# Reordering the lists of three engines in the first dispatch block of a layer-norm, linear-attention and soft-mixture kernel

## The reference

```
o   = (q k^T / sqrt(C)) v          # no softmax; q, k, v from a layer-normed x
x   = x + ln(ln(x) + o proj + b)   # first sublayer
x3  = ln(x)                        # second sublayer
logits   = einsum('bmd,dnp->bmnp', x3, phi)           # 64 experts x 32 slots
dispatch = softmax(logits, axis=0)                    # over the batch of 2
combine  = softmax(logits over n*p)
slots = einsum('bmd,bmnp->bnpd', x3, dispatch)
y     = einsum('bnpd,nde->bnpe', slots, W) + b
out   = einsum('bnpd,bmnp->bmd', y, combine)
x     = x + ln(out)
```

## Time and profile before

| | us |
|---|---|
| median of 3 runs | 640.99 |
| lowest and highest run | 640.54, 641.14 |
| the profiled execution | 641.88 |
| its span, from the first to the last instruction | 640.1 |
| PE busy | 628.2 |
| DVE busy | 447.9 |
| ACT busy | 359.0 |
| POOL busy | 230.2 |

### The profile page before, as it was taken

One profiled execution on the slowest core, in us unless ns is written; L12 is line 12 of the kernel. 1 busy time (PEld: TensorE's weight loads), 2 busy tenths in 40 slices (PEclk: granted clock), 3 DMA queues, 4 the chain that ended last, 5 costly groups with the idle time before them and its releaser, 6 DMA issues.

```text
span 640.1 us, 15341 instructions
## 1 busy us (share of the span) xinstructions
PE 628.2 (98%) x5351; PEld 395.4 (62%) x5351; DVE 447.9 (70%) x857; ACT 359.0 (56%) x694; POOL 230.2 (36%) x410
## 2 busy tenths in 40 slices
PE   8999999999999999999999999999999999999996
PEld 8898644545444444444444457777777777777776
DVE  5978888835244453446344399999888888888886
ACT  5666776843233232224444356777777777777764
POOL 5375896820000000000000001555555555555554
PEclk9999999999999999999999999999999999999999
DMA  8920032325766666666555531222222222222201
GB/s 266 402 77 1 1 67 50 67 60 156 201 176 176 177 193 185 173 178 203 135 136 186 159 104 67 91 90 90 90 90 90 90 90 90 90 90 90 90 16 34
DMA packets 78485, 77.07 MB, mean 120 GB/s; under 512 B 6386, under 2 KB 74995, under 8 KB 76147
## 3 DMA queue, kind: packets, MB, share of 16 engines
q1 hardware_dynamic: 76112, 74.48, 38.4%
q10 hardware_dynamic: 2338, 2.16, 1.0%
HBM read 51.71 MB, written 23.07 MB: 117 GB/s over the span
## 4 chain that ended last, share of the span: by engine, by line
PE 79%; DVE 8%; POOL 5%; issue 3%; DMA 2%; ACT 2%; SPq 1%; DVEq 0%; POOLq 0%; ACTq 0%
PE psL L1568 24%; PE psM L1555 11%; PE psL L1687 11%; PE psM L1705 7%; PE psM L1709 7%; PE psM L1706 7%; PE psM L1585 3%; POOL small L492 2%; DMA r_xn<-in_proj_wT 2%; PE psL L1773 1%; PE psL L1453 1%; PE psM L1511 1%; DVE phs L1091 1%; DVE small L1286 1%; DVE r_xn L1305 1%
## 5 line engine op out<-in xcount | busy, mean ns | idle before, releaser
L1568 PE MATMUL psL<-r,r_xn 128*128 128x512 f16 x768 | 176.3, 379 | 0.8 <-DVE r L1112 0.8
L1568 PEld LDWEIGHTS psL<-r,r_xn 128*128 128x128 f16 x768 | 73.4, 98 | 91.0 <-issue 7.0
L762 ACT ACTIVATE r<-psM,small 128x512 f32<-128x512 f32 x64 | 43.7, 682 | 96.3 <-PE psM L1555 95.5
L1555 PE MATMUL psM<-phs,xx 128*128 128x512 f16 (+1 forms) x384 | 93.2, 379 | 0.9 <-DVE xx L1146 0.9
L580 POOL MEMSET r_xn<- 128x8 f16 x2 | 0.3, 137 | 234.2 <-PE psL L1568 234.2
L1110 DVE TENSOR_SCALAR r<-r 128x512 f16<-128x512 f32 x64 | 28.5, 445 | 71.8 <-ACT r L762 71.8
L1687 PE MATMUL psL<-phs,r 128*32 128x512 f16 x1344 | 75.1, 379 | 0.0
L1555 PEld LDWEIGHTS psM<-phs,xx 128*128 128x128 f16 x384 | 37.3, 98 | 45.9 <-DVE xx L1146 1.4
L875 ACT ACTIVATE r<-psL,small 128x512 f32<-128x512 f32 x60 | 41.9, 776 | 37.7 <-DVE small L1313 37.4
L492 POOL TENSOR_TENSOR small<-small,epst 128x2 f32<-128x2 f32 (+3 forms) x75 | 59.8, 797 | 6.2
L1687 PEld LDWEIGHTS psL<-phs,r 128*32 128x32 f16 x1344 | 34.6, 97 | 36.5 <-issue 3.0
(11 more groups left out here) (200 smaller groups left out, 1260.8 us busy)
## 6 DMA issues: line engine op xcount, KB each, us to landing
r<-in_ffn_w SPq DMA_DIRECT2D x23, 1024.0 KB, 5.8
logit_difference<-r SPq DMA_DIRECT2D x256, 64.0 KB, 1.9
xx<-logit_difference SPq DMA_DIRECT2D x16, 1024.0 KB, 4.8
out<-r SPq DMA_DIRECT2D x32, 128.0 KB, 1.7
xres<-in_x SPq DMA_DIRECT2D x7, 512.0 KB, 11.4
r<-in_phi SPq DMA_DIRECT2D x1, 2048.0 KB, 19.3
expert_bias<-r ACTq DMA_DIRECT2D x1, 2048.0 KB, 21.6
r<-expert_bias SPq DMA_DIRECT2D x16, 128.0 KB, 5.5
```

The lines of the kernel that those rows point to most:

```text
L1555: ins = mm(bk[j % 2][:, :].rearrange("p (q m) -> p q m", q=EP), xxT[:, 1, j, hx, k, :], phw[:, hp, k, :, bass.ds(nb, 1), :].rearrange("p q ...
L1568: ins = mm(psL[:, i * 512:(i + 1) * 512], x3n[:, b, j, hx, k * P:(k + 1) * P], thl[:, j % 2, hs, :], start=(j == 0 and hx + hs == 0), stop ...
```

## The change

It changes the order of steps in three lists. No step is added, removed or altered.

- ACT: y_squares(1, 5) moves behind tanh(0, 0); xd_hi(1) moves ahead of x3_float(0, 2) and d_copy(0, 0); tanh(0, 3) and xd_hi(2) move ahead of x3_float(0, 3).
- DVE: residual(1, 2) moves behind add_x(0, 6), xd_diff(1) and split(0, 0).
- PE: d_first(5) moves ahead of turn_xd(3), slots_first(6) ahead of turn_xd(4).

```diff
@@ ACT
-            x3_float(0, 1); xd_hi(0); x3_hi(0, 1); y_squares(1, 4); x3_float(1, 1); y_squares(1, 5)
-            act.wait_ge(phi_split, 1); tanh(0, 0); x3_float(0, 2); d_copy(0, 0); xd_hi(1); tanh(0, 1)
+            x3_float(0, 1); xd_hi(0); x3_hi(0, 1); y_squares(1, 4); x3_float(1, 1)
+            act.wait_ge(phi_split, 1); tanh(0, 0); y_squares(1, 5); xd_hi(1); x3_float(0, 2); d_copy(0, 0); tanh(0, 1)
             x3_hi(1, 1); d_copy(0, 1); x3_hi(0, 2); y_squares(0, 6); tanh(0, 2); x3_float(1, 2)
-            d_copy(0, 2); x3_hi(1, 2); x3_float(0, 3); tanh(0, 3); xd_hi(2); d_copy(0, 3)
+            d_copy(0, 2); x3_hi(1, 2); tanh(0, 3); xd_hi(2); x3_float(0, 3); d_copy(0, 3)
@@ DVE
             add_x(0, 5); xd_diff(0); stats_x2(1, 1); add_x(1, 4); stats_x2(0, 2); xd_lo(0)
-            add_x(1, 5); residual(1, 2); add_x(0, 6); xd_diff(1); split(0, 0); stats_x2(1, 2)
+            add_x(1, 5); add_x(0, 6); xd_diff(1); split(0, 0); residual(1, 2); stats_x2(1, 2)
@@ PE
             d_first(0); d_first(1); turn_xd(1); slots_first(0); d_first(2); slots_first(1)
-            d_first(3); turn_xd(2); slots_first(2); d_first(4); slots_first(3); turn_xd(3)
-            d_first(5); slots_first(4); d_first(6); slots_first(5); h_pair(1, 6); d_first(7)
-            turn_xd(4); slots_first(6); h_pair(1, 7); d_first(8); slots_first(7); turn_xd(5)
+            d_first(3); turn_xd(2); slots_first(2); d_first(4); slots_first(3); d_first(5)
+            turn_xd(3); slots_first(4); d_first(6); slots_first(5); h_pair(1, 6); d_first(7)
+            slots_first(6); turn_xd(4); h_pair(1, 7); d_first(8); slots_first(7); turn_xd(5)
```

## The result

The changed kernel takes 642.12 us (median of 22 runs, 641.56 to 642.84), the kernel before 641.11 (22 runs, 640.54 to 641.62). The ratio is 1.0016, 95% interval 1.0009 to 1.0022: 1.0 us slower, 0.1 us above the range that was given, in the direction that was not forecast. By the bound of 0.2% it is no change that counts, but with 22 runs on each side it is a clear one. Of all timed runs in this document one was slow, a run of e3_after_pool of 815.45 us at a granted clock of 0.753, and its ratio leaves it out.

A forecast was written before the change was run, and what follows sets the result against it. PE, busy 98%, waited 3.46 us ahead of 110 us on a chain through POOL, ACT and DVE. Most gains were taken back at slots_first(4) and (9), leaving 0.3: 641.88 less 0.3, less 0.89, is 640.7 us, range 639.3 to 642.0.

The forecast's parts named there:

- the sum: Whole kernel: profiled execution 641.88 us, less 0.3 gained, less 0.89 to reach the timed runs' median, gives 640.7.
- The 0.89: Excess in us of the profiled execution, 641.88, over the timed median, 640.99; subtracted from the forecast as well.
- T: On POOL: end of its x3 terms of (1,3), 92.2 us before; nothing in the change moves what precedes, collisions may.
- I take +0.3: At T: forecast delay in us from collisions, since three added ones can be named and two that end.
- The bound of +1.4: At T: the latest shift allowed in us, if three net collisions are added; it gave the range's slow end.
- rival 4: DVE work moved forward hits POOL's pieces, 4 net collisions of 0.45: T + 1.8, 642.5 us; chance 0.09.
- Three or four collisions of 0.45 are added and about as many end elsewhere: Up to T: moved DVE instructions lengthen POOL's small pieces by 0.45 us each, roughly balanced by collisions that end.
- The waits of PE: First block: old waits go, new ones ahead of turn_xd(2) 0.7, slots_first(4) about 1.5, slots_first(9) 0.3 to 0.8 us.
- 0.13 saved behind T: From T to split(0,4)'s end: 5.07 us instead of 5.2, so the terms of (0,4) start only 0.15 later.
- it keeps the lead to the end: PE behind slots_first(9): the lead left there, taken as 0.2 to 0.3 us, lasts to the kernel's end.
- This is the part that can pay: PE at turn_xd(4): slots_first(6) going first removes a 0.99 us wait; lead 0.84 at d_first(8), limited at slots_first(9).
- rival 3: All 3.46 us of PE idle time ahead of 110 us is won, giving 637.5 us; chance 0.03.

The follow-up runs named there:

- e3_after_pool: Changed kernel with POOL's x3_terms(1,3) moved ahead of x3_lo(0,2) and y_terms(0,6) behind x3_lo(1,3); 640.79 us, ratio 0.9995.
- e3_after_tie: Changed kernel with two memsets on DVE, each waited for, ahead of split(0,1); 641.39 us, ratio 1.0005.
- e2_before_pool_late: Kernel before with one memset of a column on POOL ahead of y_terms(1,5); 642.23 us.

## Why the prediction was wrong, point by point

- **The step that failed** is the one under the sum. All durations were taken from one profiled execution, and the sum ended with "It lies 0.89 over the median of the three runs, 640.99, which with the same term becomes 640.7". The 0.89 was treated as a constant of profiling. It was a different course of the same kernel: the profiled execution lay 0.74 us above the slowest of the three timed runs, the second one (640.67) did not, and its rest was 1.08 us shorter. T of before is 16.51 in the common course, not 17.63. Against the traced course the change wins 0.12 us in the rest; against the common one it loses 1.08 - 0.12 = 0.96, and the timed runs show 1.0.
- **The size of T**, the term of the sum that this hits. "I take +0.3": against the trace it was +0.24 (17.63 to 17.87), against the common execution +1.36. The hit is luck: in the trace of before POOL had lost the pair of split(0,1) and y_terms(1,5), as it does in every trace of the changed kernel, so its cost dropped out of the comparison. The bound of +1.4 would have held +1.36, had it been laid on the right base; it is the mechanism of rival 4 ("POOL becomes later"), at a price of 1.0 us instead of 1.5.
- **The collisions were counted, not ordered.** The prediction said: "Three or four collisions of 0.45 are added and about as many end elsewhere". Which of two nearly simultaneous instructions goes first was not looked at. The one at split(0,1) and y_terms(1,5), under 0.02 us apart in the first trace of before, was worth 0.6 us of the time and 0.84 up to the last matmul in the changed kernel (e3_after_tie), and 1.1 to 1.3 in before (e2_before_pool_late).
- **The waits of PE** were right but for one: turn_xd(1), slots_first(0), turn_xd(2) (a new wait, 0.48; 0.7 was said), d_first(4), slots_first(4) (1.45; 1.5), turn_xd(4), slots_first(9) (0.46; 0.3 to 0.8). The one ahead of turn_xd(3) was to go and stayed, at 0.25. The statement was right that what is won up to slots_first(3) comes together as one wait at slots_first(4).
- **What stands behind T** was mis-sized too, within the traced course. The three x3_lo took 3.83 us instead of 4.23, 0.4 less, where the sum had 0.13 saved behind T. So the terms of (0,4) start 0.15 us earlier from the first product (23.75 against 23.90), where 0.15 later was said.
- **"it keeps the lead to the end"** failed by the larger part: 0.32 us of lead at slots_first(9), 0.12 in the rest. The difference goes at turn_xd(7), which no row of the prediction looked at. That the span came out 0.3 us shorter, as forecast, is for two thirds the earlier first product.
- **"This is the part that can pay"**, of the swap of slots_first(6) and turn_xd(4): alone, with turn_xd(3)'s, it gave at most 0.1 us in the rest (564.48 to 564.37) and nothing in the timed runs. PE's lead was taken back ahead of slots_first(9), as the prediction had it, and behind it.
- **"All idle time is won"**, rival 3, fell. The runs show a part of what it would have taken: the chain from stats_x2(0,4) had to be freed, which the change doesn't touch, and that brought 1.4 us of the 3.46.

Not settled: why one chip shows before's longer course in perhaps a third of its runs and another in none. And that the runs of before over 641.9 us are this course was not seen in a trace of each, only in the two traces of before and in the kernel that forces it. Nor is it settled why the change without its edit of DVE's list, where POOL wins the pair, is as slow as the whole change.

## What to carry to other kernels

Hold the profiled execution against the timed runs before anything is read from it: one that lies outside their range by as much as the change is worth, as here, may be another course of the program, and a second trace comes first. Where two engines hold each other up and one of them is on the path, look in the timeline for pairs that start within 0.03 us, and give both outcomes; a reordering that seems to free an engine may only turn such a pair round. And look for a step that stands behind something it does not need, ahead of a long chain: moving stats_x2(0,4) and x3_terms(0,4) brought 1.4 us, where the waits that the change freed brought none.

## What the runs showed of the hardware

- A delay of 0.07 us on POOL (a memset of 0.10 us) made the kernel 1.1 us (at the last matmul) to 1.3 us (in the medians) slower, and a delay of 0.15 us on DVE made it 0.6 us faster, both where the order of one pair of instructions turned round with it.
- In that pair a DVE instruction of 0.42 us on SBUF held POOL's from 0.19 to 0.45 to 0.48, or was itself 0.45 instead of 0.42 where POOL's shorter one came 0.02 us before it. In 18 traces POOL's instruction was held where it started up to 16 ns ahead or behind, and was not where it started 19 ns or more ahead.
- DVE instructions that read one input from PSUM (line 1103, 0.84 us for two beside an x3_lo) were not held up in the first trace of before: all 32 of them took 0.45 to 0.48 us.
- A memset of one column on DVE, 0.06 us, placed between xd_lo and split in the changed kernel cost nothing: split started at 5.89 after the first product with it and without it.
